# The rest channels of a normalised token: turned once and copied by ScalarE, in a float32 windowed-attention kernel

## The reference, cut to what matters

```python
x = _ln(x, ln1g, ln1b)                      # mean and variance over 160 channels
qkv = xw @ qkvw + qkvb                      # xw: the tokens by windows
attn = softmax(q @ k.T * HEAD_DIM ** -0.5 + bias + mask)
x = sc + (attn @ v) @ projw + projb
h = _ln(x, ln2g, ln2b)
x = x + gelu(h @ w1 + b1) @ w2 + b2
```

## Time and profile before

| | before |
|---|---|
| median of 3 runs | 3090.34 us (3089.7 to 3090.7) |
| span of the profiled execution | 3089.1 us |
| TensorE (PE) busy | 2989.3 us, 97% |
| TensorE weight loads (PEld) busy | 2698.0 us, 87% |
| VectorE (DVE) busy | 2223.4 us, 72% |
| ScalarE (ACT) busy | 1715.3 us, 56% |
| GpSimd (POOL) busy | 827.8 us, 27% |
| mean granted TensorE clock | 0.988 of full speed |
| one body of block 1, G0 to G0 | 40.87 us |
| one body of block 2, G0 to G0 | 44.37 us |

### The profile page before, as it was taken

How to read it: one execution, slowest core, us unless ns; L and a number is a source line. 1 busy time by engine, 2 the same in 40 slices (tenths; PEclk the granted TensorE clock), 3 DMA queues, 4 the chain that set the end, 5 groups by cost and what they waited for, 6 DMA issues and landing times. The chain is left out here.

```text
span 3089.1 us, 102841 instructions
## 1 busy us (share of the span) xinstructions
PE 2989.3 (97%) x39898; PEld 2698.0 (87%) x39898; DVE 2223.4 (72%) x6736; ACT 1715.3 (56%) x4076; POOL 827.8 (27%) x1470
## 2 busy tenths in 40 slices
PE   8889999999999999999999999999999999999799
PEld 6679888898888888898888888888888889888699
DVE  5667777777777777777777777777777777777422
ACT  6456656666655656666555655565556555655321
POOL 8122222222222222222232233223322332232110
PEclk9989999999999999999999999999999999999899
DMA  6411111111111111113111111111111111112284
GB/s 142 155 60 41 38 34 39 30 35 39 39 39 39 39 33 39 31 34 93 44 39 29 33 40 33 29 37 40 33 26 40 40 33 26 40 40 42 43 141 82
DMA packets 210425, 147.29 MB, mean 48 GB/s; under 512 B 15955, under 2 KB 205206, under 8 KB 210332
## 3 DMA queue, kind: packets, MB, share of 16 engines
q1 hardware_dynamic: 207619, 142.41, 19.7%
q10 hardware_dynamic: 1008, 3.44, 0.5%
q0 software_dynamic: 1728, 0.48, 0.1%
HBM read 95.64 MB, written 52.50 MB: 48 GB/s over the span
## 5 line engine op out<-in xcount | busy, mean ns | idle before, releaser
L1543 PE MATMUL rm<-w,ht 128*112 128x160 f32 x4480 | 682.7, 302 | 0.0
L1543 PEld LDWEIGHTS rm<-w,ht 128*112 128x112 f32 x4480 | 611.8, 177 | 5.2
L1029 POOL TENSOR_TENSOR rs<-ln_tmp,mhalf 112x4 f32<-112x4 f32 (+1 forms) x128 | 119.1, 931 | 1625.0 <-DVE ln_tmp L1201 1624.9
L1119 ACT ACTIVATE ht<-rm 128x448 f32<-128x448 f32 (+1 forms) x640 | 319.0, 498 | 193.4 <-PE rm L127 193.4
L1084 ACT ACTIVATE vb<-ra 113x320 f32<-113x320 f32 x256 | 113.1, 442 | 278.4 <-PE ra L127 276.8
L127 PE MATMUL rm<-z2t_hi,w_hi 128*128 128x448 f32 (+1 forms) x640 | 257.2, 402 | 4.4 <-DVE z2t_rest L1309 3.3
L987 POOL TENSOR_TENSOR z<-z,one 112x448 f32<-112x448 f32 (+2 forms) x192 | 131.3, 684 | 354.9 <-DVE z L1205 354.9
L127 PE MATMUL rm<-z2t_rest,w_rest 98*128 98x448 f32 (+1 forms) x640 | 219.9, 344 | 0.0
L127 PE MATMUL rm<-z2t_lo,w_hi 128*128 128x448 f32 (+1 forms) x640 | 219.1, 342 | 0.0
L127 PE MATMUL rm<-z2t_hi,w_lo 128*128 128x448 f32 (+1 forms) x640 | 218.2, 341 | 0.0
L1248 DVE TENSOR_TENSOR sc<-so,tabs 113x490 f32<-113x490 f32 x256 | 171.3, 669 | 54.8 <-PE so L1489 42.5
(11 more groups left out here) (258 smaller groups left out, 8848.5 us busy)
## 6 DMA issues: line engine op xcount, KB each, us to landing
xa<-xs SPq DMA_DIRECT2D x128, 245.0 KB
xr<-xs SPq DMA_DIRECT2D x128, 245.0 KB
xs<-xo SPq DMA_DIRECT2D x64, 245.0 KB
ys<-yz SPq DMA_DIRECT2D x64, 245.0 KB
c_y<-ys SPq DMA_DIRECT2D x36, 260.0 KB
xs<-a_tok SPq DMA_DIRECT2D x14, 560.0 KB, 6.6
xs<-tok_late SPq DMA_DIRECT2D x14, 560.0 KB, 6.8
a_nat<-in_x ACTq DMA_DIRECT2D x7, 480.0 KB, 6.4
```

The lines of the kernel that those rows point to most:

```text
L1029: gp.tensor_tensor(rs[1][:, t0:t0 + nt], ln_tmp[1][5][:, t0:t0 + nt], mhalf[:, 0:nt], ALU.pow).then_inc(s_pow, 1)
L1119: act_(ht[:, f * SN + t0 * TT:f * SN + (t0 + nt) * TT], bank_m(i, lm, use)[:, 0:nt * TT], ACT.Gelu_apprx_tanh).then_inc(m_freed(i, lm, use ...
L1543: last = mm(bank_m(i, lm, use)[0:TT, t * DIM:(t + 1) * DIM], ht[:, c:c + TT], keep.w["w2", lm][:, f * DIM:(f + 1) * DIM], start=(f == 0), ...
```

## The change

The normalised tokens are 160 wide again. `repeat_rest` is gone with its semaphores, so TensorE waits for the normalisation itself. The turning of C has 32 channels. ScalarE evicts these 32 rows twice: to partitions 0 to 31, then to 64 to 95, and signals behind the second. VectorE's subtraction reads PSUM and the high part at partitions 0 to 31 and writes 32 to 63.

```diff
-            def repeat_rest(t, s, t0=0, nt=ST):
-                once = view(t, 0, TT, t0 * ZW + 128, [[ZW, nt], [0, 2], [1, REST]])
-                gp.tensor_tensor(view(t, 0, TT, t0 * ZW + DIM, [[ZW, nt], [REST, 2], [1, REST]]), once,
-                                 view(one, 0, TT, 0, [[0, nt], [0, 2], [0, REST]]), ALU.mult).then_inc(s, 1)
...
-                    for part, dst, rows in (("A", z1t[0], 128), ("C", z1t[2], CR)):
+                    for part, dst, rows, places in (("A", z1t[0], 128, (0,)), ("C", z1t[2], REST, (0, 2 * REST))):
                         use = f"T1{part}{hf}"
                         act.wait_ge(*a_full(i, use))
-                        act_(view(dst, 0, rows, t0 * WIN, [[WIN, nt], [WP, 16], [1, WIN]]),
-                             view(bank_a(i, use), 0, rows, 0, [[TT, nt], [WIN, 16], [1, WIN]]), ACT.Copy).then_inc(s_hi1, 1)
+                        for p0 in places:
+                            last = act_(view(dst, p0, rows, t0 * WIN, [[WIN, nt], [WP, 16], [1, WIN]]),
+                                        view(bank_a(i, use), 0, rows, 0, [[TT, nt], [WIN, 16], [1, WIN]]), ACT.Copy)
+                        last.then_inc(s_hi1, 1)
...
-                    for part, dst, rows in (("A", z2t[0], 128), ("C", z2t[2], CR)):
+                    for part, dst, rows, places in (("A", z2t[0], 128, (0,)), ("C", z2t[2], REST, (0, 2 * REST))):
...
-                                        view(bank_a(i, use), p0, rows, 0, [[TT, nt], [WIN, 16], [1, WIN]]),
-                                        view(src, p0, rows, t0 * WIN, dims).bitcast(F32),
+                                        view(bank_a(i, use), 0, rows, 0, [[TT, nt], [WIN, 16], [1, WIN]]),
+                                        view(src, 0, rows, t0 * WIN, dims).bitcast(F32),
...
-                for part, f0, rows in (("A", 0, 128), ("C", 128, CR)):
+                for part, f0, rows in (("A", 0, 128), ("C", 128, REST)):
...
-                        pe.wait_ge(s_z[0], i + 2)
+                        pe.wait_ge(s_norm[0], i + 2)
```

More of the change, by code:

```diff
@@ L725, in phase_b @@
         xo, yz = sb("xo", [TT, ST * DIM]), sb("yz", [TT, ST * DIM])
-        z1, z2 = sb("z1", [TT, ST * ZW]), sb("z2", [TT, ST * ZW])
+        z1, z2 = sb("z1", [TT, ST * DIM]), sb("z2", [TT, ST * DIM])
         st = [sb(f"st{n}", [TT, ST * 6]) for n in range(2)]
@@ L730, in phase_b @@
         half, mhalf, by_dim, eps = sb("half", [TT, ST]), sb("mhalf", [TT, ST]), sb("by_dim", [TT, ST]), sb("eps", [TT, ST])
-        one = sb("one", [TT, 1])
         ln_tmp = [[sb(f"ln_tmp{n}_{k}", [TT, ST]) for k in range(8)] for n in range(2)]
@@ L761, in phase_b @@
         s_norm = [sem("norm1"), sem("norm2")]
-        s_z = [sem("z1_full"), sem("z2_full")]
         s_hi1, s_hi2, s_oth = sem("z1t_hi_done"), sem("z2t_hi_done"), sem("ot_hi_done")
@@ L983, in inv_std @@
                 assert len(steps) == RS_STEPS[0]
-            def repeat_rest(t, s, t0=0, nt=ST):
-                once = view(t, 0, TT, t0 * ZW + 128, [[ZW, nt], [0, 2], [1, REST]])
-                gp.tensor_tensor(view(t, 0, TT, t0 * ZW + DIM, [[ZW, nt], [REST, 2], [1, REST]]), once,
-                                 view(one, 0, TT, 0, [[0, nt], [0, 2], [0, REST]]), ALU.mult).then_inc(s, 1)
-            for t, c in ((half, 0.5), (by_dim, 1.0 / DIM), (eps, EPS), (one, 1.0)):
+            for t, c in ((half, 0.5), (by_dim, 1.0 / DIM), (eps, EPS)):
                 gp.memset(t[:], c)
@@ L1015, in body @@
                     inv_std(i + 1)
-                if ln is not None:
-                    pool.wait_ge(s_norm[0], i + 2)
-                    repeat_rest(z1, s_z[0])
                 if lm is None and la is None:
@@ L1029, in body @@
                         gp.tensor_tensor(rs[1][:, t0:t0 + nt], ln_tmp[1][5][:, t0:t0 + nt], mhalf[:, 0:nt], ALU.pow).then_inc(s_pow, 1)
-                        pool.wait_ge(s_norm[1], 2 * i + hf + 1)
-                        repeat_rest(z2, s_z[1], t0, nt)
                         if la == 1:
@@ L1106, in t_hi @@
                     t0, nt = HALF[hf]
-                    for part, dst, rows in (("A", z2t[0], 128), ("C", z2t[2], CR)):
+                    for part, dst, rows, places in (("A", z2t[0], 128, (0,)), ("C", z2t[2], REST, (0, 2 * REST))):
                         use = f"T2{part}{hf}"
                         act.wait_ge(*turned_full(n, lm, use))
-                        act_(dst[0:rows, t0 * TT:(t0 + nt) * TT], turned_bank(n, lm, use)[0:rows, 0:nt * TT],
-                             ACT.Copy).then_inc(s_hi2, 1)
+                        for p0 in places:
+                            last = act_(dst[p0:p0 + rows, t0 * TT:(t0 + nt) * TT], turned_bank(n, lm, use)[0:rows, 0:nt * TT],
+                                        ACT.Copy)
+                        last.then_inc(s_hi2, 1)
                 if lm is not None:
@@ L1204, in normalise @@
                 for t in range(t0, t0 + nt):
-                    ins = v.tensor_scalar(z[:, t * ZW:t * ZW + DIM], x_[:, t * DIM:(t + 1) * DIM],
+                    ins = v.tensor_scalar(z[:, t * DIM:(t + 1) * DIM], x_[:, t * DIM:(t + 1) * DIM],
                                           mean[n][:, t:t + 1], rs[n][:, t:t + 1], ALU.subtract, ALU.mult)
@@ L1304, in t_lo @@
                     cols = slice(t0 * TT, (t0 + nt) * TT)
-                    for k, (part, dst, src, rows) in enumerate((("A", z2t[1], z2t[0], slice(0, 128)),
-                                                               ("C", z2t[2], z2t[2], slice(REST, 2 * REST)))):
+                    for k, (part, dst, src, p0, rows) in enumerate((("A", z2t[1], z2t[0], 0, 128),
+                                                                   ("C", z2t[2], z2t[2], REST, REST))):
                         use = f"T2{part}{hf}"
                         dve.wait_ge(s_hi2, hi2(n, 2 * hf + k + 1))
-                        v.tensor_tensor(dst[rows, cols], turned_bank(n, lm, use)[rows, 0:nt * TT], src[rows, cols].bitcast(F32),
+                        v.tensor_tensor(dst[p0:p0 + rows, cols], turned_bank(n, lm, use)[0:rows, 0:nt * TT],
+                                        src[0:rows, cols].bitcast(F32),
                                         ALU.subtract).then_inc(turned_freed(n, lm, use)[0], 1)
@@ L1428, in turn @@
                     for t in range(nt):
-                        c = (t0 + t) * ZW + f0
+                        c = (t0 + t) * DIM + f0
                         last = tr(bank_of(use)[0:rows, t * TT:(t + 1) * TT], z[:, c:c + rows], keep.ident[0:TT, 0:TT])
@@ L1575, in body @@
                     mlp_in(range(3))
-                    pe.wait_ge(s_z[1], 2 * m + 2)
+                    pe.wait_ge(s_norm[1], 2 * m + 2)
                     mlp_turned(m, 1)
@@ L1656, in body @@
                 if la is not None:
-                    pe.wait_ge(s_z[1], 2 * i + 1)
+                    pe.wait_ge(s_norm[1], 2 * i + 1)
                     mlp_turned(i, 0)
```

## The result

The changed kernel takes 3265.07 us (median of 4 runs, 3264.6 to 3265.98), the kernel before 3090.52 on the same chip: a ratio of 1.0561, 95% interval 1.0546 to 1.0576. The forecast was 3124 with a range of 3097 to 3131, and the direction alone was right. The loss is 174.5 us where 34.4 were worked out.

The account below looks back on a forecast made before the run. TensorE, busy 97%, was taken as the bound, so only its waits count. Block 1's 16.3, block 2's 18.6 and −0.5 for one-offs gave +34.4 on the 3089.1 span, with 1.2 to the median: 3124, range 3097 to 3131.

Parts of the forecast that it names:

- GpSimd's copies: Removing 192 copies: 0.1 us won of 0.61 at block 1's body end, nothing in block 2, −0.5 for one-offs.
- Costed at nothing: Items priced zero: second eviction in the MLP turning's second half, second `pt`, and VectorE's subtraction with moved partitions.
- Front of block 1: Start of block 1's bodies: TensorE waits 0.30 us for `pt`, and Q0 comes later, 0.36 in all, 32 times.
- front of block 2: Start of block 2's bodies: TensorE waits 0.30 us for `pt`, 30 times; Q0's slack takes the second half's delay.
- end of a body in block 2: Second eviction delays VectorE's subtraction ahead of G0 from 1785.44 to 1785.75: +0.31 us, 31 times.
- The end in block 1: Second eviction delays VectorE's subtraction ahead of G0 from 984.43 to 984.58: +0.15 us, 32 times.
- C2: ScalarE's second eviction of the 32 rows, taken as not overlapping its neighbours: spacing of length plus 0.01 us.
- the term for one-offs: Outside the steady loops, removing GpSimd's copies was taken as −0.5 us, bounds −1 and +0.5.
- B: Rival: ScalarE's second eviction overlaps like most evictions; +11.4 us, so 3102; chance 0.20.
- C: Rival: turning fewer channels makes TensorE's transposes faster, some 43 us; some 3082, or 3059; chance 0.05.
- D: Rival: nothing to be seen, the second eviction hidden in ScalarE's idle time; 3090; chance 0.05.
- E: Rival: turning 32 columns switches TensorE's way of working, 108 us on top; 3232; chance 0.03.

Follow-up runs that it names:

- experiment 1: Changed kernel, with GpSimd waiting for VectorE's normalisation of a half before block 2's base work: 3126.47 us, ratio 1.0136 to the kernel before.
- experiment 3: Changed kernel, with only the second of GpSimd's two base operations per half in block 2 waiting for the normalisation: 3206.79 us, ratio 1.0375.
- experiment 4: Changed kernel, block 2's base work waiting for normalisation, plus an unread GpSimd product on its own tile beside the first half's normalisation: 3216.67 us, ratio 1.0421.
- experiment 5: Changed kernel, with 13 added TensorE products, results unread, where the linear's third part waits for `yz` in block 2: 3200.6 us, ratio 1.0366.
- experiment 7: Changed kernel, block 2's base work waiting for normalisation, ScalarE's second eviction written to partition 0 of its own tile: 3101.02 us, ratio 1.0024.

## Why the prediction was wrong

**The failed step: "GpSimd's copies".** It costs the removal by what TensorE waits for: the 0.61 us of the copy and how much earlier the turning begins. Of block 2 it says that nothing is won, and takes it that nothing can be lost. It never asks what stands behind the copy on GpSimd's own queue. That is the base work of block 2, and what goes with the copy is also GpSimd's wait for VectorE, 1.29 us long in the kernel before. Experiments 1, 3 and 4 show the rest: base work beside the normalisation, four tiles at 3.45 for 1.18, the linear 2.3 us later, 31 times. No term, no bound and no rival of the prediction has GpSimd and VectorE meet; "Costed at nothing" lists ScalarE's and VectorE's edits and not this one.

**The second omission: what a new wait does to the clock.** With a right delay the sum would have been 34.4 + 31 × 2.27 = 104.8, so 3195, near the 3200.6 of experiment 5. The other 65 us come from the granted clock behind each wait of 2.7 us. In the kernel before, the linear's wait was 0.44, and the clock stood at 1.00 in the steady bodies; no row of the prediction prices this.

**What held.** With the collision taken away (experiment 1) the bodies come out nearly term by term. Front of block 1 +0.34 for +0.36, front of block 2 +0.31 for +0.30, end of a body in block 2 44.98 − 44.68 = +0.30 for +0.31. The end in block 1 was mis-sized: 41.31 − 41.21 = +0.10 for +0.15, 1.6 us in all. G0's waits for `z2t_rest` are 47.4 us for the 44 forecast, TensorE's for `pt` 14.1 for 18. C2 is serial, as taken, and its doubt is settled by experiment 7. That the spans too differ by 33.5 (3122.6 − 3089.1) for 34.4 is in part luck: the term for one-offs, −0.5, was wrong. The first G0 comes 3.0 us later and the end behind the last G0 takes 1.6 more, but the last body is 2.8 shorter (41.50 for 44.28), since its mean clock was 1.00 where the kernel before had 0.88.

**The rivals.** B (C2 overlaps) did not happen, but its price was right when it was made to: 44.59 − 44.37 = 0.22 in block 2 for 0.24, and 0.00 in block 1 for 0.14, 31 × 0.22 = 6.8 us (0.24% of the time measured, 7.4) for 11.4. C (shorter turning) would have shown in block 1 and didn't. D (nothing to be seen) fell with G0, whose waits grew. E (another way of working of TensorE) had the nearest time, 3232, for a reason that the runs exclude: in experiment 1 the same narrow turning stands, and the loss is gone. That so large a time lay there was chance.

## What to carry to other kernels

When an instruction is taken from an engine's queue, its wait goes too: read what stood behind it there, when that will now run, and beside what. Here a copy that seemed to cost only time kept GpSimd from working while VectorE normalised. And a new wait of TensorE is to be priced with the granted clock behind it; where a wait can't be avoided, filling it can pay (65 us here). A gain found in passing (one wait that covers two uses) is worth trying by itself: nothing else tried here made the kernel faster than it was before the change.

## What the runs showed of the hardware that was not expected

VectorE's normalisation, 112x160 between SBUF tiles, goes from 1.18 us for four in a row to 2.90 when one instruction of GpSimd of 2.05 started 0.06 ahead, and GpSimd is not slowed. Two evictions of ScalarE whose outputs start at different partitions do not overlap, where those with the same start overlap by 0.10 (experiment 7).

TensorE's granted clock was at 0.50 for 6.8 us at each of the changed kernel's steady waits of 2.7 us. A longer wait did not mean a longer fall: behind the waits of 2.15 in experiment 4 it lasted 3.4 us in 27 of 30 bodies, behind those of 1.37 in experiment 3 it lasted 6.8 in 23 of 30, 3.4 in one, and was absent in six. In the steady bodies with waits of 0.44 it never fell. What decides between these is left open. So is why the first G0 comes some us earlier or later from kernel to kernel (208.7 before, 211.8 in experiment 1).
